# Row statistics of the second feed-forward stage taken inside the attention loop, and its routing begun one step sooner

## The reference

```
x = x + 0.5 * ffn(layernorm(x))
x = x + attn(layernorm(x))
x = x + 0.5 * ffn(layernorm(x))
```

## Time and profile before

| | us |
|---|---|
| median of 3 | 1429.34 (1428.12 to 1429.48) |
| the profiled execution, its own time | 1430.07 |
| its span | 1428.3 |
| PE busy | 1268.3 (89%) |
| POOL busy | 972.8 (68%) |
| DVE busy | 896.4 (63%) |
| ACT busy | 628.5 (44%) |

### The profile page before, as it was taken

How to read it: one execution, slowest core, us unless ns; L and a number is a source line. 1 busy time by engine, 2 the same in 40 slices (tenths; PEclk the granted TensorE clock), 3 DMA queues, 4 the chain that set the end, 5 groups by cost and what they waited for, 6 DMA issues and landing times.

```text
span 1428.3 us, 23451 instructions
## 1 busy us (share of the span) xinstructions
PE 1268.3 (89%) x6920; PEld 1095.2 (77%) x6920; DVE 896.4 (63%) x2190; ACT 628.5 (44%) x1092; POOL 972.8 (68%) x1348
## 2 busy tenths in 40 slices
PE   5793999999996789999999999977699999999990
PEld 5593888888885568888888888866588888888880
DVE  5764722254657987878778786866685622354553
ACT  2143334434434456666565566553243334434420
POOL 3578882284876687978879797831588881484866
PEclk9796999999998899999999999998899999999995
DMA  9975565587754200010000000111355566687653
GB/s 350 408 292 170 198 242 185 198 266 240 264 190 167 77 31 16 31 46 16 31 16 30 15 30 30 61 52 45 141 203 192 198 231 214 217 274 244 224 171 114
DMA packets 86921, 218.44 MB, mean 153 GB/s; under 512 B 16272, under 2 KB 28560, under 8 KB 85904
## 3 DMA queue, kind: packets, MB, share of 16 engines
q1 hardware_dynamic: 62224, 149.82, 29.4%
q0 software_dynamic: 24576, 67.14, 14.7%
HBM read 109.43 MB, written 107.48 MB: 152 GB/s over the span
## 4 chain that ended last, share of the span: by engine, by line
PE 46%; DVE 17%; POOL 16%; issue 14%; DMA 4%; ACT 2%; POOLq 0%; DVEq 0%; SPq 0%; ACTq 0%; another core or an unknown queue 0%
PE ps L1116 12%; POOL f_gbuf L516 7%; PE ps L1150 6%; POOL xg L490 5%; PE ps L1082 4%; PE ps L2101 4%; DVE at_xs L1898 4%; PE ps L2103 3%; PE ps L2102 3%; PE ps L1121 3%; PE ps L2162 2%; DMA f_gbuf<-yg,f_rows 2%; PE ps L1132 1%; PE ps L2187 1%; PE ps L2151 1%
## 5 line engine op out<-in xcount | busy, mean ns | idle before, releaser
L516 POOL DMA_INDIRECT f_gbuf<-yg,f_rows x256 | 266.5, 1041 | 190.5 <-DMA yg<-f_yo 136.7
L490 POOL DMA_INDIRECT xg<-f_xn,f_rows x256 | 252.3, 986 | 88.7 <-issue 55.7
L1116 PE MATMUL ps<-f_wgu,f_xT 128*128 x1248 | 296.6, 381 | 0.0
L1116 PEld LDWEIGHTS ps<-f_wgu,f_xT 128*128 128x128 f32 x1248 | 225.7, 191 | 24.9 <-issue 0.3
L858 DVE TENSOR_TENSOR f_h<-ps,f_sg 128x256 f32<-128x256 f32 x156 | 66.0, 423 | 228.1 <-ACT f_sg L573 227.5
L573 ACT ACTIVATE f_sg<-ps 128x256 f32<-128x256 f32 x156 | 59.8, 383 | 316.7 <-PE ps L1116 314.8
L890 DVE SCALAR_TENSOR_TENSOR f_xin<-f_gbuf,f_w,f_xin 128x256 f32<-128x256 f32 x256 | 128.1, 500 | 80.8 <-DMA f_gbuf<-yg,f_rows 73.7
L1150 PE MATMUL ps<-f_wd,f_hT 128*128 x624 | 161.5, 381 | 7.2 <-DVE f_hT L866 7.2
L1898 DVE SCALAR_TENSOR_TENSOR at_xs<-at_raw,at_taps,at_xs 128x512 f32<-128x512 f32 x136 | 135.6, 999 | 6.5 <-POOL at_xs L1548 3.8
L560 ACT COPY f_xT<-ps 128x512 f32<-128x512 f32 x216 | 125.5, 581 | 32.1 <-PE ps L1082 23.2
L1121 PE MATMUL ps<-f_xT,f_wgu_sh 128*128 128x256 f32 x512 | 128.2, 401 | 11.7 <-DVE f_hT L862 11.7
(11 more groups left out here) (261 smaller groups left out, 2713.9 us busy)
## 6 DMA issues: line engine op xcount, KB each, us to landing
f_xq<-xg SPq DMA_DIRECT2D x78, 512.0 KB, 4.8
yg<-f_yo SPq DMA_DIRECT2D x156, 256.0 KB, 2.8
xg<-f_gbuf SPq DMA_DIRECT2D x39, 512.0 KB, 6.7
f_wgu<-in_gate_up SPq DMA_DIRECT2D x4, 1280.0 KB, 13.2
f_xin<-in_x SPq DMA_DIRECT2D x8, 512.0 KB, 7.4
xg<-f_xn,f_rows POOLq DMA_INDIRECT x256
f_gbuf<-yg,f_rows POOLq DMA_INDIRECT x256, 3.7
x<-f_xin SPq DMA_DIRECT2D x8, 512.0 KB, 3.3
```

Of the source, the lines that this page charges most:

```text
L490: G.indirect_dma_start(xg[0:USED[g] * P, :], bass.IndirectOffsetOnAxis(ap=rows[g][:, b, k:k + 1], axis=0), xn[:, SUB * TILE0[g] + b, :], N ...
L516: G.indirect_dma_start(gbuf[:, n % GBUF, k, :], None, yg[0:USED[g] * P, :], bass.IndirectOffsetOnAxis(ap=rows[g][:, b, k:k + 1], axis=0), ...
L1116: last = T.matmul(gu_ps[:, j % 2, s * 2 * P:(s + 1) * 2 * P], x_of(k, s, d), weight(wgu[:, :, d, :], experts[s]), start=(d == 0), stop=(d ...
```

## The change

`statistics_out` is new: behind each output sum of chunks 0 to 27 DVE takes one `bn_stats` of it, into `bn_out`, and f2's `statistics(t)` for tiles 0 to 6 only aggregates those. The four aggregations no longer wait for one another, in both stages. f2 reads and writes its tiles in the order in which attention holds them, so each DMA piece is 1 KB instead of 4 KB. The generator's pieces on DVE stand earlier: tiles 0 to 2 in tile 6, q=0; tiles 3 and 4 at q=1; tile 5 at q=2; tile 6 in tile 7, q=0. GpSimd's memsets stand behind the residual bias of tile 6, q=0, and its rstd of tiles 0 to 6 go in three instructions ahead of the scatters. `route_piece(0, 0)` and `(0, 1)` stand ahead of X_lo(30), as does ScalarE's `squash(0)`; TensorE's `turn_x` and `router` pieces come one hook sooner. Four of f2's events change places, and DVE's duties at them move one event earlier.

```diff
@@ -332,8 +330,9 @@
     chain = sem("chain")
 
     xg, yg = scratch["xg"], scratch["yg"]
-    src_v = src.rearrange("(t p s) d -> t p s d", p=P, s=SUB)
-    dst_v = dst.rearrange("(t p s) d -> t p s d", p=P, s=SUB)
+    token_order = "(t p s) d -> t p s d" if fresh else "(t s p) d -> t p s d"
...
@@ -460,23 +459,29 @@
         G.memset(half_neg[:], -0.5).then_inc(init_done, 1)
         G.memset(seg_long[:], 1.0).then_inc(init_done, 1)
         G.memset(seg_short[:], 1.0).then_inc(init_done, 1)
-        G.memset(sign[:], 1.0).then_inc(init_done, 1)
-        pool.wait_ge(init_done, 4)
+        if fresh:
+            G.memset(sign[:], 1.0).then_inc(init_done, 1)
+        pool.wait_ge(init_done, 3 + fresh)
         if fresh:
             G.memset(blank, 0.0).then_inc(init_done, 1)
         G.memset(seg_long[:, :, 0:1], 0.0).then_inc(init_done, 1)
         G.memset(seg_short[:, :, 0:1], 0.0).then_inc(init_done, 1)
-        G.memset(sign[:, E - 1::E], 1.0 - E).then_inc(init_done, 1)
-        pool.wait_ge(init_done, 7 + fresh)
+        if fresh:
+            G.memset(sign[:, E - 1::E], 1.0 - E).then_inc(init_done, 1)
+        pool.wait_ge(init_done, 8 if fresh else 5)
 
         yield
 
         def rstd_of(t):
             pool.wait_ge(var_ready, t + 1)
             G.tensor_tensor(rstd[:, t], var[:, t], half_neg[:], ALU.pow).then_inc(rstd_ready, 1)
-            if not fresh:
-                pool.wait_ge(rstd_ready, t + 1)
-                G.tensor_tensor(nbias[:, t], nbias[:, t], rstd[:, t], ALU.mult).then_inc(nbias_ready, 1)
+
+        def rstd_of_tiles(a, b):
+            pool.wait_ge(var_ready, b)
+            G.tensor_tensor(rstd[:, a:b], var[:, a:b], half_neg[:].unsqueeze(1).broadcast_to([P, b - a, SUB]),
+                            ALU.pow).then_inc(rstd_ready, b - a)
+            pool.wait_ge(rstd_ready, b)
+            G.tensor_tensor(nbias[:, a:b], nbias[:, a:b], rstd[:, a:b], ALU.mult).then_inc(nbias_ready, b - a)
 
         rests = [0]
...
@@ -526,15 +531,22 @@
             for t in range(4):
                 rstd_of(t)
         else:
-            for t in range(3):
-                rstd_of(t)
-                yield
+            rstd_of_tiles(0, 3)
+            yield
+
+            rstd_of_tiles(3, 6)
+            yield
+
+            rstd_of_tiles(6, 7)
+            G.memset(sign[:], 1.0).then_inc(init_done, 1)
+            pool.wait_ge(init_done, 6)
+            G.memset(sign[:, E - 1::E], 1.0 - E).then_inc(init_done, 1)
+            yield
 
             pool.wait_ge(rows_ready, 1)
             scatter(0, 0)
             yield
 
-            rstd_of(3)
         next(other, None)
         scatter_group(0, 0 if fresh else 1)
...
@@ -665,11 +677,17 @@
 
         def statistics(t):
             new_chain()
-            dve.wait_ge(x_in[t], 16)
+            if fresh or t == NT - 1:
+                dve.wait_ge(x_in[t], 16)
+                for s in range(SUB):
+                    link(V.bn_stats(bn[:, s, :], xin[:, t, s, :]))
+                of = bn
+            else:
+                dve.wait_ge(attn["stats_taken"], SUB * (t + 1))
+                of = attn["bn_out"][:, SUB * t:SUB * (t + 1), :]
             for s in range(SUB):
-                link(V.bn_stats(bn[:, s, :], xin[:, t, s, :]))
-            for s in range(SUB):
-                link(V.bn_aggr(mv[:, t, s, :], bn[:, s, :]))
+                ins = V.bn_aggr(mv[:, t, s, :], of[:, s, :])
+            link(ins)
             if not fresh:
                 V.tensor_scalar(nbias[:, t], mv[:, t, :, 0], -1.0, None, ALU.mult)
...
@@ -916,8 +936,9 @@
         for g in range(GROUPS):
             V.memset(later[:, g:g + 1], float(GROUPS - 1 - g))
         link(V.memset(seek_of[:], SENTINEL))
-        dve.wait_ge(init_done, 7 + fresh)
-        dve.wait_ge(small_in, 32)
+        dve.wait_ge(init_done, 8 if fresh else 5)
+        if fresh:
+            dve.wait_ge(small_in, 32)
         def first_duties(kind, n):
 
...
@@ -995,24 +1012,30 @@
             shift_of(3)
         else:
             statistics(1)
-            yield
-
             statistics(2)
             yield
 
-            for i in range(3):
+            statistics(3)
+            statistics(4)
+            yield
+
+            statistics(5)
+            yield
+
+            statistics(6)
+            yield
+
+            dve.wait_ge(small_in, 32)
+            for i in range(2):
                 route_piece(0, i)
-                yield
+            yield
+
+            route_piece(0, 2)
+            yield
 
             copy_counts(0, START)
             route_piece(0, 5)
             route_piece(0, 6)
-            yield
-
-            statistics(3)
-            yield
-
-            statistics(4)
             yield
...
@@ -1415,6 +1439,7 @@
             settle(sp)
             of = tile_of(src_v, t)
             after(sp, "stored", 16 * t)
+            after(sp, "stats_taken", SUB * t)
             sp.dma_start(x_res[:], of).then_inc(s["res_in"], 16)
 
         def tile(t, par):
...
@@ -1627,10 +1650,8 @@
                     first_tap(t + 2, par, 0)
                 if q == 1 and more(t, 2):
                     rstd_of(t + 2)
-                if q == 1 and isinstance(t, int) and t == NT - 2:
+                if q < SUB - 1 and isinstance(t, int) and t == NT - 2:
                     next(after_it, None)
-            if isinstance(t, int) and t == NT - 2:
-                next(after_it, None)
 
         pairs_of_tiles(pool, tile)
 
@@ -1819,9 +1840,12 @@
                     else:
                         round_X(c + 1)
                         silu_z(c + 1)
-                        if q < 2:
+                        if q < 1:
                             next(after_it, None)
                 else:
+                    if isinstance(t, int) and t == NT - 2:
+                        settle(act)
+                        next(after_it, None)
                     if more(t, 1):
                         silu_x(t + 1, nx, 2 * q + 1)
                     if more(t, 2):
@@ -1911,6 +1935,11 @@
             dve.wait_ge(s["out_in_psum"], c + 1)
             dve.wait_ge(s["res_biased"], t + 1)
             V.tensor_tensor(x_res[:, q, :], xu_ps[:, 0, 0:D], x_res[:, q, :], ALU.add).then_inc(s["out_added"], 1)
+
+        def statistics_out(c, q):
+            dve.wait_ge(s["out_added"], c + 1)
+            at = bass.ds(c, 1) if not isinstance(c, int) else slice(c, c + 1)
+            V.bn_stats(bn_out[:, at, :].rearrange("p o n -> p (o n)"), x_res[:, q, :]).then_inc(s["stats_taken"], 1)
 
         def rest_of_X(c):
...
@@ -2065,35 +2091,38 @@
                         add_out(t - 1, c - 1, SUB - 1)
                     if q == 2:
                         add_out(t, c - 1, q - 1)
-                    if q in (0, 2) and not more(t, 1):
-                        next(after_it, None)
                     if q == 0 and more(t, 2):
                         statistics(t + 2)
+                    if q == 0 and not start:
+                        statistics_out(c - 1, SUB - 1)
+                    if q > 0 and more(t, 1):
+                        statistics_out(c - 1, q - 1)
+                    if not more(t, 1):
+                        next(after_it, None)
+                    if q < SUB - 1 and isinstance(t, int) and t == NT - 2:
+                        next(after_it, None)
                     if q == 1 and more(t, 1):
                         rest_of_g(t + 1, nx)
                     if q == 2 and more(t, 2):
                         normalize(t + 2)
                     rest_of_X(c + 1)
-                    if q == 1 and not more(t, 1):
-                        next(after_it, None)
                 else:
                     if more(t, 2):
                         rest_of_xT(t + 2, par)
                     if more(t, 1):
                         convolve(t + 1, nx, 2 * q + 1)
                     add_out(t, c - 1, q - 1)
+                    if not more(t, 1):
+                        settle(dve)
                     statistics_y(c)
                     if more(t, 1):
                         rest_of_X(c + 1)
-                    else:
-                        settle(dve)
-                        next(after_it, None)
-            if isinstance(t, int) and t >= NT - 2:
+                        statistics_out(c - 1, q - 1)
+            if isinstance(t, int) and t == NT - 1:
                 next(after_it, None)
 
         pairs_of_tiles(dve, tile)
         rest_of_ynT(SUB * NT - 1)
-        next(after_it, None)
...
```

72 lines of the change are left out of this document (35 added, 37 removed).

## The result

The changed kernel takes 1438.41 us in the median of 5 runs (1433.71 to 1440.14), the kernel before 1429.34 (1427.81 to 1431.91) beside it: a ratio of 1.0052, interval 1.0033 to 1.0072. It is slower, by 9.1 us where +3 (1432) was forecast. That is inside the range of 1420 to 1439 by 0.6 us, and outside the forecast's own range of 1428 to 1437.

The account below looks back on a forecast made before the run. TensorE was taken to bound the attention loop and the routed part, VectorE's queue the 990 to 1020 us stretch. +3.5 + 9.5 + 2.0 + 1.5 − 12.7 − 0.8 = +3.0: 1433.1 profiled, 1432 median; range 1420 to 1439.

Parts of the forecast that it names:

- The wait for the constants: Tile 6, q=0: VectorE stands some 10.6 us until GpSimd's constants are set, delaying X_lo(25) and TensorE; +9.5, bounds 0 and 12.
- the lower clock: Tile 6: after the long wait TensorE's matmuls restart at a lower clock; +1.5 us, bounds 0 and 1.7.
- Two aggregations in q=1: Tile 6, q=1: two aggregations and the wait on the statistic's sign delay X_lo(26); +2.0 us, bounds 0.7 to 3.
- The statistic in the loop: Attention tiles: one added statistic per tile delays X_lo at q=1, seven tiles at 0.5 us; +3.5, bounds 0 and +7.
- Rival B: Loop pays in more than one step a tile as VectorE's spare time ahead of X_lo runs out; 1436, chance 0.17.
- a period more than 0.8 us longer: Attention loop: tile periods this much longer were named as a sign that the forecast was wrong.
- The routing: Second stage's start: earlier sums, ranks and scatters bring the routed part forward; −12.7 us, bounds −6.8 and −15.
- −10.9 at chunk 31: Chunk 31's output product begins earlier, 8.0 us from the routing and 2.9 from tile 3's removed statistics.
- The −1.75 at the gathered rows: Start of the routed part: TensorE's 1.75 us wait for the first gathered rows goes, since the scatters win 14.8.
- the regrouped events of the second stage keep the same work: 0: Second stage: moving its events and duties costs nothing; 0, bounds −1 and +1 us.
- First stage −0.8: First stage: unlinked aggregations shorten TensorE's first wait for VectorE; −0.8 us, bounds 0 and −1.5.
- token order 0: Second stage's loads and stores in 1 KB instead of 4 KB pieces cost nothing; 0, bounds −0.4 and +1 us.

Follow-up runs that it names:

- normalise first: Changed kernel with VectorE's wait for the constants moved to their first reader and, in q=2, the new statistic behind the normalisation: 1425.61 us, 0.9967 of before.
- short pad: Kernel before plus two memsets of 168 columns ahead of the normalisation in q=2, tiles 0 to 5: 903.4 us from first sum to end, one run.
- first trace: Profiled execution of the changed kernel, the quickest of its five runs: span 1431.7 us, 911.4 from chunk 0's output sum to the end.
- second trace: Profile of the changed kernel run again without edit: span 1435.4 us, 911.5 from chunk 0's output sum to the end; median 1438.32, ratio 1.0068.
- old events: Changed kernel with the wait for the constants later and the second stage's events, duty places and later counts as before: 1427.72 us, 0.9980 of before.

## Why the prediction was right or wrong

**The wait for the constants: right.** The 10.6 us without work on VectorE were 10.49, the reason was GpSimd's memsets behind the residual bias, and X_lo(25) came 10.0 us late counted from the sum ahead (forecast 10.35). TensorE waited 8.94 us and then lost some 1.4 at the lower clock, +9.5 and +1.5 in the sum. Without this wait the kernel is at 0.9996: it cost what the whole change lost.

**Two aggregations in q=1: right in itself, wrong in the sum.** +2.0 was forecast. The statistic and the aggregations do take 1.7 us of VectorE's queue (913.97 to 915.69), but X_lo(26) is no later than X_lo(25) was (+10.1 against +10.0), so nothing was added. During the stall ScalarE and GpSimd had got ahead: ynT_lo(24), for which VectorE waited 2.40 us before, was there at once (it waits 2.13 for TensorE one instruction later), and the convolution's two operations took 1.53 us instead of 2.81, with GpSimd idle beside them. With the stall taken away 1.6 to 1.8 appear. Costs in consecutive steps don't add where the first has let the other engines get ahead, and the sum added them. Tile 6: +9.9 to +10.4 instead of +13.5.

**The statistic in the loop: mis-sized.** The failed step is "So I charge one statistic per tile": +3.0 for these six tiles, where +7.0 was measured. The queue part is right: "normalise first" costs 62.5 to 62.7 a tile, 0.3 to 0.4 above before. The other 1.2 to 1.3 in each of tiles 2 to 5 are none of the statistic's own time; they are the normalisation, held beside GpSimd. I looked at VectorE's queue ahead of X_lo and at idle time, and not at what an engine next door was doing at the moment to which the following instructions moved. Rival B named the amount (+3.5 more), q=2 as the step that pays, and the sign of it, a period more than 0.8 us longer, all of which came. Its mechanism, that the statistic uses up the spare time, did not: the short pad's 0.4 us cost nothing, and "normalise first" has the same queue without the cost.

**The routing: mechanism right, some 4 us short in all.** Of −12.7 up to the gathered rows, −8.1 and −8.6 came. Of the −10.9 at chunk 31 the first trace gives −8.4, the second −10.5, of which 1.6 are the clock between chunks 27 and 28 (0.91 in the trace of before). The 2.9 us of tile 3's statistics came in full; the counts came 5.4 us earlier in the first trace where I had 8.0. X_lo(30) waits behind sums for which the scores come 3.12 us late; I had the sums ready. The −1.75 at the gathered rows came and was taken again, by the new wait for f_hT (1.4 us more than the longest before) and by the lower clock behind it (some 1.6 in the first trace, twice that in the second): "the regrouped events of the second stage keep the same work: 0" is the step that failed, as far as the wait goes; the cause of the lower clock is open. With the old events −11.5 of the −12.7 are there (81.4 + 66.2 against 91.5 + 67.6).

**First stage −0.8, token order 0:** inside what the runs can tell.

The sum by the second trace: +7.1 + 10.4 − 10.5 + 1.9 − 0.5 = +8.4, where I had +3.8 for the same stretches. Two misses of about 4 us (loop, routing with its new wait) went in one direction, one of 3 in the other. That they left the result just inside the range is luck; that the kernel is slower, and by which wait, was foreseen.

## What to carry to other kernels

When a piece of another stage is put into a queue earlier, read its first wait, and ask when the engine that answers it does so there; a wait for constants belongs beside their first reader. What an added instruction costs is not its length: look at which instructions of VectorE and GpSimd start together behind it, since here 0.1 us decided about a microsecond in each round of a loop. And count from a mark behind the part that varies, here the first output sum, before two traces are compared.
